# A decoder layer on one core: context tile 14, two norm chains, the row terms and one copy of c2 change places

## The reference

```python
x = x + attn(layernorm(x), Wqkv, bqkv, Wo, bo)      # one head of 256
x = x + matmul(fake_quant(layernorm(x)), fake_quant(ctx))   # ctx: 1024 x 1024 per sequence
x = x + ffn(layernorm(x), c1_w, c2_w, w1, w2t)
# fake_quant(x) = (clip(round(x / s + z), 0, 255) - z) * s
# ffn: inter = x @ c1.T @ c2.T (rank 16, 3584 wide); in each block of 64 the
#      position of the maximum is taken; h = relu(w1[idx] . x); out = h @ w2t[idx]
```

## Time and profile before

| what | before |
|---|---|
| median of three runs | 799.47 us |
| the profiled execution | 799.37 us |
| its span | 797.5 us |
| TensorE busy | 786.5 us (99%) |
| VectorE busy | 592.7 us (74%) |
| GpSimd busy | 433.4 us (54%) |
| ScalarE busy | 249.4 us (31%) |
| granted TensorE clock | 1.0 in all stretches |

### The profile page before, as it was taken

One profiled execution on the slowest core, in us unless ns is written; L12 is line 12 of the kernel. 1 busy time (PEld: TensorE's weight loads), 2 busy tenths in 40 slices (PEclk: granted clock), 3 DMA queues, 4 the chain that ended last, 5 costly groups with the idle time before them and its releaser, 6 DMA issues.

```text
span 797.5 us, 11473 instructions
## 1 busy us (share of the span) xinstructions
PE 786.5 (99%) x3883; PEld 640.0 (80%) x3888; DVE 592.7 (74%) x963; ACT 249.4 (31%) x374; POOL 433.4 (54%) x265
## 2 busy tenths in 40 slices
PE   8999999999999999999999999999999999999998
PEld 7888887468788888888888888888888888888886
DVE  5655568877984878787777878787878777777864
ACT  5457567872321131212122120303121212212030
POOL 3935797675999954544525253445454443525240
PEclk9999999999999999999999999999999999999999
DMA  8126403000111011111111111101111111111104
GB/s 333 71 101 215 162 1 106 8 1 8 60 53 30 31 53 60 53 59 53 59 53 59 53 59 53 45 16 50 59 53 59 53 59 53 59 53 53 53 15 196
DMA packets 22615, 53.22 MB, mean 67 GB/s; under 512 B 4544, under 2 KB 6592, under 8 KB 22464
## 3 DMA queue, kind: packets, MB, share of 16 engines
q1 hardware_dynamic: 22448, 51.86, 18.9%
q10 hardware_dynamic: 144, 1.05, 0.4%
HBM read 48.70 MB, written 4.19 MB: 66 GB/s over the span
## 4 chain that ended last, share of the span: by engine, by line
PE 87%; DVE 8%; DMA 2%; POOL 1%; ACT 1%; issue 1%; SPq 0%; DVEq 0%
PE bank L1752 12%; PE bank L1753 12%; PE bank L1754 12%; PE bank L1657 11%; PE bank L1659 11%; PE bank L1658 11%; PE bank L1470 3%; PE bank L1472 3%; PE bank L1471 3%; PE bank L1611 2%; PE bank L1666 2%; PE bank L1648 2%; DMA x<-x_in 1%; PE bank L1627 1%; DVE stats L1024 1%; PE bank L1486 1%
## 5 line engine op out<-in xcount | busy, mean ns | idle before, releaser
L1752 PE MATMUL bank<-w_hi,h_hi 128*128 128x512 f32 x448 | 176.5, 394 | 1.5 <-DVE x L1258 1.5
L1753 PE MATMUL bank<-w_lo,h_hi 128*128 128x512 f32 x448 | 175.1, 391 | 0.0
L1754 PE MATMUL bank<-w_hi,h_lo 128*128 128x512 f32 x448 | 174.5, 390 | 0.0
L1261 DVE TENSOR_TENSOR x<-bank,x 128x512 f32<-128x512 f32 x208 | 133.5, 685 | 50.0 <-PE bank L1754 50.0
L562 POOL TENSOR_TENSOR lo_r<-r,slot 128x512 fp32r<-128x512 f32 x52 | 67.5, 1300 | 160.4 <-ACT slot L785 160.4
L1754 PEld LDWEIGHTS bank<-w_hi,h_lo 128*128 128x128 f32 x448 | 84.1, 188 | 18.0
L1752 PEld LDWEIGHTS bank<-w_hi,h_hi 128*128 128x128 f32 x448 | 84.1, 188 | 17.9 <-DVE x L1258 2.2
L1753 PEld LDWEIGHTS bank<-w_lo,h_hi 128*128 128x128 f32 x448 | 84.4, 188 | 15.2
L1657 PE MATMUL bank<-xT_hi,slot 128*128 128x512 f32 x240 | 95.0, 396 | 0.0
L1658 PE MATMUL bank<-xT_lo,slot 128*128 128x512 f32 x240 | 93.5, 390 | 0.0
L1659 PE MATMUL bank<-xT_hi,lo_r 128*128 128x512 f32 x192 | 74.8, 390 | 0.0
(11 more groups left out here) (203 smaller groups left out, 1600.3 us busy)
## 6 DMA issues: line engine op xcount, KB each, us to landing
r<-w SPq DMA_DIRECT2D x56, 256.0 KB, 3.4
w_raw<-w SPq DMA_DIRECT2D x28, 512.0 KB, 4.0
x<-x_in SPq DMA_DIRECT2D x8, 512.0 KB, 10.4
ctx_raw<-ctx_in SPq DMA_DIRECT2D x8, 512.0 KB, 4.0
xn<-ctx_in SPq DMA_DIRECT2D x8, 512.0 KB, 5.5
out<-x SPq DMA_DIRECT2D x7, 512.0 KB, 2.7
W_raw<-wqkv SPq DMA_DIRECT2D x6, 512.0 KB, 10.8
c_raw<-c SPq DMA_DIRECT2D x112, 16.0 KB, 2.0
```

Source lines behind the costliest of these rows:

```text
L1261: nc.vector.tensor_tensor(x[:, t, c], bank[unit_banks(g)[p]][:, :], x[:, t, c], ALU.add).then_inc(unit_added, 1)
L1752: nc.tensor.matmul(dst, h_hi[:, j, m], w2_hi[:, j, c], start=j == 0, stop=False)
L1753: nc.tensor.matmul(dst, h_hi[:, j, m], w2_lo[:, j, c], start=False, stop=False)
L1754: last = nc.tensor.matmul(dst, h_lo[:, j, m], w2_hi[:, j, c], start=False, stop=j == GJ - 1)
```

## The change

On GpSimd one of the sums of the context tiles (`add_q2(0, 4)`) moves ahead of the conversions of tiles 14 and 15. On ScalarE and VectorE the second value bank and the first two transposed probability tiles go ahead of context tile 14, and tile 15 goes behind all four. On VectorE the sum of product 1 goes ahead of the norm chain of tiles 6 and 7, and the first norm chain of round 2 ahead of the sum of product 5; on ScalarE the copy of q1T 4 goes ahead of the norm of tile 6. `row_biases` moves from behind `cut_c2(1)` to behind `cut_c2(0)`. The copy in `cut_c2(1)` becomes an operation of ScalarE between its four h copies of group 0, with a semaphore of its own, and VectorE keeps the subtraction.

```diff
@@ gpsimd @@
                 if i == KD + 3:
                     add_q2(0, 3)
-            add_q2(0, 4)
+                if i == KD + 5:
+                    add_q2(0, 4)
             add_q2(0, 5)
@@ scalar @@
             scale_ctx(12)
             scale_ctx(13)
-            scale_ctx(14)
             hi_V(1, 1)
             act.wait_ge(mm_done, nth("V", 1, 1) + 1)
             act.dma_start(Wo_raw[:, :, :], wo).then_inc(Wo_loaded, 16)
+            hi_PT(0, 0)
+            hi_PT(0, 1)
+            scale_ctx(14)
+            hi_PT(0, 2)
+            hi_PT(0, 3)
             scale_ctx(15)
-            for i in range(TB):
-                hi_PT(0, i)
...
             centre_q1(5)
+            copy_q1T(4)
             norm(1, 6)
-            copy_q1T(4)
             norm(1, 7)
...
-            for c in FIRST_ORDER:
-                hi_h(0, *c)
+            hi_h(0, *FIRST_ORDER[0])
+            hi_h(0, *FIRST_ORDER[1])
+            act.wait_ge(c2_loaded, 2 * 16 * SLOTS)
+            act.wait_ge(score_done, PAIRS)
+            nc.scalar.activation(c2_stack[:, :], c2_raw[:, :], ACT.Copy).then_inc(c2_hi_done, 1)
+            hi_h(0, *FIRST_ORDER[2])
+            hi_h(0, *FIRST_ORDER[3])
@@ vector @@
+            def late_c2():
+                half = slice(P // 2, P)
+                dve.wait_ge(c2_hi_done, 1)
+                nc.vector.tensor_tensor(c2_stack[half, :], c2_raw[half, :], c2_stack[half, :].bitcast(F32),
+                                        ALU.subtract).then_inc(c2_done, 1)
...
             round_ctx(13)
+            lo_V(1, 1)
+            lo_PT(0, 0)
+            lo_PT(0, 1)
             round_ctx(14)
-            lo_V(1, 1)
+            lo_PT(0, 2)
+            lo_PT(0, 3)
             round_ctx(15)
...
-            for i in range(TB):
-                lo_PT(0, i)
...
             round_q1(5)
+            add_XA(1)
             norm_scale(1, 6)
-            add_XA(1)
             copy_CB(1)
...
             add_XA(4)
+            norm_scale(2, 0)
             add_XA(5)
-            norm_scale(2, 0)
             add_XA(6)
...
             cut_c2(0)
+            row_biases()
...
             dve.wait_ge(score_done, PAIRS)
-            cut_c2(1)
-            row_biases()
+            late_c2()
             lo_h(0, 0, 1)
```

More of the change, by code:

```diff
@@ L313, in decoder_layer @@
         c2_done = sem("c2_done")
+        c2_hi_done = sem("c2_hi_done")
         score_done = sem("score_done")
```

## The result

| what | before | after |
|---|---|---|
| median | 799.47 us (5 runs) | 794.32 us (5 runs) |
| ratio | | 0.9935, 95% interval 0.9919 to 0.9951 |
| the profiled execution | 799.37 us | 794.16 us |
| its span | 797.5 us | 792.3 us |
| TensorE busy | 786.5 us | 785.7 us |

The account below looks back on a forecast made before the run. TensorE, busy 99% of the span, was taken to bound the kernel, with only nine waits, 6.7 us, to win. 1.45 + 0.5 + 1.75 = 3.7 us off 799.37 gave 795.7; the 8-in-10 range was 794.4 to 797.4.

Parts of the forecast that it names:

- Part 3: Row terms and c2 copy leave VectorE's queue in group 0, ending the wait at output unit 6; 1.75 us won.
- I take 1.75: Gain at output units 6 and 10 of group 0, in us; bounds 1.3 and 1.85.
- Part 2: Reordered sums, norm chains and q1T copy start products 3 and 7 earlier; 0.5 us, between 0 and 1.36.
- So the rounding of tile 6 ends at about 153.75: VectorE's rounding, ready 0.13 us behind GpSimd's addition, waits for the shared port and ends there instead of at 151.2.
- move together: VectorE, ScalarE and GpSimd, released by TensorE behind a removed wait, were taken to shift with it.
- rival 1: Rounding of tile 6 gets the port first, or GpSimd comes later; sums and norm chains bring 1.36, 794.8 us; chance 0.20.
- Part 1: Value bank and probability tiles ahead of context tile 14 remove two score waits; 1.45 us, bounds 0.8 and 1.57.
- Rivals 2 and 3: 2: tile 6's late rounding and Wo's cut cost gains, 797.1, chance 0.10; 3: GpSimd last at group 2, 797.4, chance 0.06.
- Rival 4: Roundings of tiles 6 and 7 each lose the port for one more addition; TensorE loses 4.7, 800.9 us; chance 0.04.

Follow-up runs that it names:

- after, held at tile 3: Changed kernel with GpSimd's first correction addition held until tile 3 is rounded; median 794.1 us, ratio to before 0.9937.
- the run that loses it once at tile 6: Changed kernel; tile 6's rounding waits for a flag GpSimd sets right ahead of its fifth correction addition; median 795.73 us.
- the two held kernels: Changed kernel with GpSimd's first correction addition held until tile 3 is rounded, 794.1 us; the same with its fifth held until tile 6 is rounded, 793.45 us.
- before, tile 3 waits: Kernel before, with the rounding of tile 3 waiting for the end of GpSimd's first correction addition; median 801.67 us.
- part 3 alone: Kernel before with only the row terms moved and the c2 copy put on ScalarE; median 796.92 us.
- before, loses once: Kernel before; tile 3's rounding waits for a flag GpSimd sets ahead of its first correction addition; median 799.69 us.
- part 2 alone: Kernel before with only the moves of VectorE's sums and norm chains and of ScalarE's q1T 4 copy; median 797.65 us.
- row terms alone: Kernel before with only the row terms moved; median 797.06 us.
- before, held: Kernel before with GpSimd's first correction addition held until tile 3 is rounded; median 798.78 us.
- ScalarE's copy alone: Kernel before with only the copy of c2 moved to ScalarE, row terms left behind VectorE's subtraction; median 797.15 us.
- the kernel with the sum moved back: Changed kernel with GpSimd's sum `add_q2(0, 4)` back behind both conversions; median 796.66 us.
- tile 6 waits for an addition: Changed kernel with the rounding of tile 6 waiting for the end of GpSimd's fifth correction addition; median 798.56 us.

## Why the prediction was wrong, point by point

The order of the parts and what each takes away were right; the sum was 1.5 too small, from four terms.

**Part 3, 1.75 for a measured 2.27.** The term "I take 1.75" was mis-sized. The cause was read rightly and the next choice started within 0.01 of the forecast. What was too small is the wait itself. The starts of TensorE's units in before give 1.54 late at unit 6 and another 0.13 at its second matmul group, 0.32 and 0.11 at unit 10 (taken as 0.1 and a restart), 0.07 at the first score pair, and a tenth in small restarts. After the change none is left, so all of it came.

**Part 2, 0.5 for 0.97.** "So the rounding of tile 6 ends at about 153.75" failed. The price of a lost port was right, and it was paid, but at tile 3. There GpSimd starts 0.22 behind VectorE's first rounding, as in before (131.50 and 131.72; 133.48 and 133.71, 0.23), and who goes first between two roundings comes out either way. The Trainium skill, page "SBUF — State Buffer", section "SBUF: two separate sides", has the loser wait for the whole instruction: the trace agrees (2.8 for 0.64). Having lost there, VectorE met no addition at tile 4 and was 0.95 late for the rest. Then the norm chain and not the q1T copy set the norm of tile 6, and its rounding came 0.15 ahead of GpSimd. For the same reason product 3 won 0.38 and not 0.74: the q1T copy of tile 3 and the sum of product 1 were late. The argument that these engines "move together" was wrong by 0.95 us, in a step whose margin was 0.13. That was rival 1 by its outcome, though not at its size of 1.36. With the port kept at both tiles (after, held at tile 3) the size is right too: 0.75 at product 3 and 0.58 from there to product 7, 1.33 against the traced before.
The 0.5 for a port lost at tile 6 alone was not measured. In the run that loses it once at tile 6 it is lost at tile 3 as well, and GpSimd's fifth addition starts 7.15 behind product 2, where it was 6.17 in before. Product 7 starts 22.57 behind product 2 there (4.27 + 18.30). With the 0.95 of tile 3 taken off, 21.62 are left, and the prediction had 22.21 - 0.5 = 21.71. By this estimate its price for that stretch was sound, and what failed is which rounding lost.

**Part 1, 1.45 for 1.61.** The cut of Wo ended in time; the chain through tile 15 was forecast 0.13 too long. It is close all the same: in the two held kernels the cut ends 0.2 and 0.3 later against the transposes than in after, and the projection starts as much later, at 14.52 and 14.66. That GpSimd's sum is needed was right: without its move the cut is 1.9 late, 2.1 were expected. But that 1.61 is near the forecast is in part luck. Eight kernels have the old order in this stretch, and the later the bias add of the second value bank starts behind the transposes, the longer it takes:

| old order | before | before, tile 3 waits | part 3 alone | before, loses once | part 2 alone | row terms alone | before, held | ScalarE's copy alone |
|---|---|---|---|---|---|---|---|---|
| bias add behind the transposes | 2.00 | 1.89 | 1.77 | 1.75 | 1.64 | 1.55 | 1.54 | 1.54 |
| part 1 | 15.93 | 15.85 | 15.68 | 15.67 | 15.58 | 15.51 | 15.46 | 15.45 |

The traced execution of before was the slowest of them. ScalarE began to scale context tile 14, for whose load it waits, 0.11 behind the transposes there and up to 0.94 ahead of them in the others. Against the middle of the eight the change brings 1.3, and 1.1 against the fastest.

**Ahead of the edits, nothing for 0.4.** The time to the first transposes varies by 1.26 us from execution to execution. The range had no term for it, nor for the one traced execution standing for all. That one was 0.95 early at product 3, 0.3 late in part 1, and had the longest stage ahead of the edits of the eight (80.12, 0.7 above their middle); its total agrees with the median because these cancel. So the miss of 0.1 below the range is itself of the size of chance: the second set of executions of the changed kernel has 794.69, inside it. The mechanisms above don't hang on that.

**Rivals 2 and 3** didn't occur: the groups behind unit 15 take the same time in both traces, and GpSimd is never waited for in group 2. **Rival 4** didn't occur by itself. In the run that imposes the loss of one more addition at tile 6 the cost was 4.3 us where it gave 4.7, but made up otherwise: one stop of 2.9 and not two, and most of the rest a lower clock behind it (see the last section), which the prediction had at nothing.

## What to carry to other kernels

When two engines meet at a port with 0.1 or 0.2 us between them, one trace doesn't say who goes first; give both outcomes their weight, or impose the order with a wait. The kernel that does so at both tiles has the lowest median here, though only its stages show the gain. Look also at how much a stage differs between executions before its length in one trace is taken as what a change can win. Size a removed wait by the starts of the waiting engine's instructions over the whole stretch, not by the idle time that is named. If two moves relieve the same wait, see whether one alone is enough before doing both.

## What the runs showed of the hardware that was not expected

**Two stops of TensorE, of 1.93 and 2.86 us, were followed by half the clock in their traces.** TensorE was busy in all of the two microseconds ahead of either stop, at a granted clock of 1.00. Windows of the kernel with the sum moved back (us, then busy time of PE, PEld, DVE, ACT, POOL, then granted clock, DMA share, GB/s), around its wait of 1.9:

```profile
108.00:110.00 2.00, 1.94 (x7) 1.61 (x8) 0.14 (x1) 1.43 (x3) 2.00 (x2) 0.85 0.00 0
110.00:112.00 2.00, 2.00 (x6) 1.52 (x6) 0.00 (x0) 0.00 (x0) 1.92 (x2) 0.50 0.00 0
112.00:114.00 2.00, 2.00 (x9) 1.59 (x8) 1.35 (x2) 0.00 (x0) 2.00 (x3) 0.80 0.00 0
114.00:116.00 2.00, 2.00 (x11) 1.64 (x10) 0.58 (x2) 1.24 (x2) 1.92 (x2) 1.00 0.00 0
```

The granted clock falls behind the stop to 0.50 (1.2 of 2.4 GHz) and is back at 1.00 from 114 on; the stage behind took 38.89 instead of 37.24: the wait of 1.9 cost 1.65 more. The same followed the stop of 2.86 where tile 6 waits for an addition (0.54 from 156 to 158, 0.61 from 158 to 160, then 1.00); the product behind it took 4.56 instead of 3.62. The stops of 1.38 and of 1.66 (the kernel before with tile 3 waiting) were followed by a full clock. What sets the border between them no run here shows, and the same program doesn't lose the clock every time. Of the four executions with the sum moved back the traced one has a mean clock of 0.997, the others have 0.999 to 1.0 and took 1.6 to 2.6 us less; of the ten where tile 6 waits, eight have 0.996 to 0.998 and two 1.0.

**A semaphore does not win a port.** VectorE, released by the end of a GpSimd operation, started 0.15 us behind the next one, which GpSimd had ready (135.73 and 135.58; 151.78 and 151.63), and waited again: 2.78 and 2.75 for a rounding of 0.64.
